# A decision-tree stage with attention threaded through it: the next group's attention one tree earlier

## Chip, core and metric

One core of a Trainium2 chip runs the whole program. The metric is the time of one execution on the device in microseconds (us); of the kernel before there are three runs, with their median. The profile is of one further execution.

## What is computed

`x` is 64 sequences of 128 rows of 128 features; `ctx` is 64 sequences of 120 rows. Four blocks follow each other, each adding to `x`; cut to what matters:

```python
x = x + cross_attention_0(layernorm(x), ctx)
x = x + mixture_of_8_experts(layernorm(x))          # top 1, and a shared expert
x = x + cross_attention_1(layernorm(x), ctx)        # softmax(q k / sqrt(128)) v
x = x + trees(layernorm(x))

def trees(x):                                       # 8 trees of depth 7, 255 nodes each
    logits = x @ W_in.T + b_in                      # 8 * 255 columns
    decisions = logits > 0
    on_path = one_hot of the 8 nodes that the decisions lead through, per tree
    return (silu(logits) * on_path) @ W_out.T
```

The layer norm in front of the second attention is called norm 3 here, the one in front of the trees norm 4 (LN4).

## The kernel before

The 64 sequences go through in 16 groups of four (`G = 4`, `W = 512` columns), so that a tile is 128 x 512 and fills one PSUM bank. A first stage does block 1 and the shared expert, a middle stage the routed experts. The last stage, `phase_c`, does the trees of group g and, between them, the second attention of group g + 1 and the norm 3 of group g + 2. It is the stage that the change touches. The group loop is unrolled for the first group and the last three, and a hardware loop of two groups a turn does the others.

**A tree on each engine.** Each group has 8 trees (`TREES`), counted by `p`, each of two chunks of 128 nodes.
- TensorE: `t_logits` gives the logits of both chunks, three 512-column matmuls each, since both operands are split into a high and a low part (`x4T_h`, `x4T_l`, `win_h`, `win_l`; lines L1009 to L1011). `t_path` adds two matmuls (L1018, L1020) of the decisions `dec` with constant matrices; they push the logit of every node off the path so far down that silu gives zero. `t_output` multiplies the masked activations with `W_out`, again split, in six matmuls (L1031 to L1033), all of a group into bank 4.
- VectorE: `t_decide` makes `dec` (L1430) of the first chunk's logits, one tree ahead; `t_low` makes the low halves `sil_l` = `sil` - `sil_h` (L1446).
- ScalarE: `t_silu_high` makes `sil` (L715) from the banks and its high halves `sil_h` (L723). For tree 1 VectorE makes the high halves. Even trees use banks 0 and 1, odd trees banks 2 and 3.

**The attention among them.** `c_scores` (L918) puts the scores in bank 7, `c_max_scores` and `c_softmax` (L654) make `prob1`, `c_turn_prob` turns it with four TensorE transposes (the helper `turn`, L758) into bank 5, `c_pT_evac` (L660) copies it to `prob1T`, `c_values` (L933) multiplies it with V into bank 6, and `c_attended` on VectorE (L1336, L1338, L1343) scales and adds it to X. `c_stats4` (L1079, L1084), `rstd` on GpSimd (L490, L492) and `c_norm4` (L1090) give the normalised rows `xn_c`. `c_turn_x4` turns them into bank 7, `c_x4_high` on ScalarE (L664) and `c_x4_low` on VectorE (L1358) split them into `x4T_h` and `x4T_l`, which the logits of the next group read. `c_stats3`, `c_norm3`, `c_turn_x` and `c_xnT_evac` (L650) do the like for norm 3 of group g + 2, through the same `xn_c` and bank 5. The output sum of a group is evacuated (`accT`, L729), turned into bank 6 in tree 3 of the group after and added to X by `t_result` (L1452).

**What sets the order.** Each engine has its own program, written out by hand: `c_body` of each engine says after which tree's step which piece of attention stands. An engine works its list in this order; between engines there are semaphore waits alone. SyncE only stores the results in this stage, and GpSimd does `rstd` and gathers the routed rows of group g + 3.

In `c_body` of TensorE the order in tree p is: logits of tree p + 1, path of tree p, output of tree p - 1. In tree 7 the first logits of the next group stand at the end. That is, between path 6 and output 6 there are output 5 and path 7 in either kernel, and in the one before the turn of norm 4's rows as well:

```python
if p == 7 and not last(g, 1):
    c_turn_x4(g + 1)
t_path(g, p)
...
if p:
    t_output(g, p - 1)
...
if p == TREES - 1 and not last(g, 1):
    t_logits(g + 1, 0)
```

Of the kernel before, what the change touches and what calls it, by code (L numbers as in the profile page):

```python
# [15 lines left out]
P = 128  # L16
# [4 lines left out]
W = G * P  # L21
# [52 lines left out]
def program(nc, x, ctx_kv, ctx_t, w0, b0, gate, sh_gate, sh_up, sh_down, rt_gate, rt_up, rt_down,  # L74
# [5 lines left out]
    with ExitStack() as ctx:  # L80
# [12 lines left out]
        V = sb("V", [KEYS, B * P])  # L93
# [38 lines left out]
        srec = sb("srec", [P, G])  # L132
# [26 lines left out]
        def bank(i, n=512, parts=P):  # L159
            return PS[0:parts, 512 * i:512 * i + n]  # L160
# [118 lines left out]
        def cols(a, start, n):  # L279

            return a[:, start:start + n] if isinstance(start, int) else a[:, bass.ds(start, n)]

        def tile(a, j, n=P):
            return a[:, j * n:(j + 1) * n]
# [16 lines left out]
        def below(g, n):  # L301

            return isinstance(g, int) and g < n

        def last(g, n):

            return isinstance(g, int) and g >= NG - n
# [23 lines left out]
        def c_bank(h, n, b):  # L331

            return 7 if below(h, n) else b
# [251 lines left out]
        def _(act):  # L585
# [145 lines left out]
            def c_body(g, u, stores):  # L731

                for p in range(TREES):
                    if p == 7 and not last(g, 1):
                        c_x4_high(g + 1)
                    t_silu_high(g, p)
                    if p == 0 and not first(g):
                        t_acc_evac(g - 1)
                    if not last(g, 1):
                        if p == 1:  # L740
                            c_softmax(g + 1)
                        if p == 3:
                            c_pT_evac(g + 1)
                    if not last(g, 2):
                        if p == 5:
                            c_xnT_evac(g + 2)
# [6 lines left out]
        def _(pe):  # L753

            def turn(dst, src, rows, n, signal):

                for j in range(G):
                    i = pe.transpose(dst[0:n, j * rows:(j + 1) * rows], tile(src, j, n), IDENT[0:rows, 0:rows])  # L758
                i.then_inc(signal, 1)
# [149 lines left out]
            def c_turn_x(h):  # L909
                pe.wait_ge(c_xn3, h + 1)  # L910
                if below(h, 2) and h:
                    pe.wait_ge(c_x4l, h)
                turn(bank(c_bank(h, 2, 5)), xn_c, P, P, c_xnT_ps)

            def c_scores(h):
# [6 lines left out]
            def c_turn_prob(h):  # L922
                pe.wait_ge(c_exp, h + 1)
                turn(bank(c_bank(h, 1, 5), W, KEYS), prob1, P, KEYS, c_pT_ps)

            def c_values(h):
                pe.wait_ge(c_pT, h + 1)
                if first(h):
                    pe.wait_ge(a_vb, V_POOL)
                if not below(h, 2):  # L930
                    pe.wait_ge(t_res, h - 1)
                for j in range(G):
                    i = pe.matmul(tile(bank(c_bank(h, 1, 6)), j), tile(prob1T, j), cols(V, h * W + j * P, P),  # L933
                                  start=True, stop=True)
                i.then_inc(c_pv_ps, 1)

# [99 lines left out]
            def c_body(g, u, stores):  # L1036
                for p in range(TREES):
                    if p == 3 and not first(g):
                        pe.wait_ge(c_x3, g + 1)
                        pe.wait_ge(t_accT, g)  # L1040
                        turn(bank(6), accT, P, P, t_acc)
                    if p + 1 < TREES:
                        t_logits(g, p + 1)
                    if p == 7 and not last(g, 1):
                        c_turn_x4(g + 1)
                    t_path(g, p)
                    if not last(g, 1):
                        if p == 0:
                            c_scores(g + 1)
                        if p == 3:  # L1050
                            c_turn_prob(g + 1)
                        if p == 4:
                            c_values(g + 1)
                    if not last(g, 2):
                        if p == 5:
                            c_turn_x(g + 2)
                    if p:
                        t_output(g, p - 1)
                    elif not first(g):
                        t_output(g - 1, TREES - 1)  # L1060
                    if p == TREES - 1 and not last(g, 1):
                        t_logits(g + 1, 0)

# [10 lines left out]
        def _(dve):  # L1074
# [259 lines left out]
            def c_attended(h):  # L1334
                dve.wait_ge(c_exp, h + 1)
                dve.tensor_reduce(ssum[:, :], by_tile(prob1, KEYS), AX.X, ALU.add).then_inc(c_sum, 1)  # L1336
                dve.wait_ge(c_sum, h + 1)
                dve.reciprocal(srec[:, :], ssum[:, :]).then_inc(c_rec, 1)  # L1338
                dve.wait_ge(c_rec, h + 1)
                dve.wait_ge(c_pv_ps, h + 1)  # L1340
                for j in range(G):
                    row = cols(X, h * W + j * P, P)
                    i = dve.scalar_tensor_tensor(out=row, in0=tile(bank(c_bank(h, 1, 6)), j), scalar=srec[:, j:j + 1],  # L1343
                                                 in1=row, op0=ALU.mult, op1=ALU.add)
                i.then_inc(c_x3, 1)

# [9 lines left out]
            def c_x4_low(h):  # L1356
                dve.wait_ge(c_x4h, h + 1)
                dve.tensor_tensor(x4T_l, bank(7), x4T_h.bitcast(F32), ALU.subtract).then_inc(c_x4l, 1)  # L1358
# [95 lines left out]
            def c_body(g, u, stores):  # L1454
                for p in range(TREES):
                    if p:
                        t_low(g, p - 1)
                    elif not first(g):
                        t_low(g - 1, TREES - 1)
                    if p + 1 < TREES:  # L1460
                        t_decide(g, p + 1)
                    elif not last(g, 1):
                        c_x4_low(g + 1)
                        t_decide(g + 1, 0)
                    if p == 3 and not first(g):
                        t_result(g - 1, 1 - u, stores)
                    if not last(g, 1):
                        if p == 1:
                            c_max_scores(g + 1)
                        if p == 4:  # L1470
                            c_attended(g + 1)
                        if p == 5:
                            c_stats4(g + 1)
                        if p == 6:
                            c_norm4(g + 1)
                    if not last(g, 2):
                        if p == 0:
                            c_add_routed(g + 2, u)
                        if p == 2:
                            c_stats3(g + 2)  # L1480
                        if p == 3:
                            c_norm3(g + 2)

            t_decide(0, 0)
            phase_c(dve, c_body)
# [42 lines left out]
```

## Time and profile before

| | |
|---|---|
| median of 3 runs | 867.29 us (867.15 to 867.87) |
| the profiled execution | 868.49 us |
| its span, first to last instruction | 866.7 us |
| last stage, from about | 385 us on |
| TensorE busy over the span | 794.8 us (92%) |
| VectorE | 653.7 us (75%) |
| ScalarE | 539.0 us (62%) |
| GpSimd | 272.3 us (31%) |

PE is TensorE and PEld its weight loads, which run beside its matmuls; DVE is VectorE, ACT ScalarE, POOL GpSimd. Matmuls are pipelined: each row's duration overlaps the next row's, so the distance between two starts is what a matmul costs. The same holds in part for VectorE and ScalarE, where an instruction starts a little ahead of the recorded end of the one before. A bracket at a row's end gives the time the engine was idle before it and who ended that.

### The profile page before, as it was taken

The numbers are of one execution on the slowest core, as the hardware profiler recorded it, in microseconds if no ns is written. First come the engines' busy times: TensorE is split into PE (matmuls) and PEld (weight loads), VectorE is DVE, ScalarE is ACT, GpSimd is POOL, SyncE is SP. The second block draws the span as 40 slices with busy tenths as digits, with TensorE's granted clock in tenths as the row PEclk, the third lists the DMA queues.
The fourth block names the chain that finished last, engine by engine and source line by source line (L and its number), as shares of the span: only waits on it lengthen the run. The fifth ranks groups of instructions, "written<-read, shape, count | busy, mean of one in ns | idle before, by whom it ended". The sixth has DMA issues, their size and how long they took to land.

```text
span 866.7 us, 15372 instructions
## 1 busy us (share of the span) xinstructions
PE 794.8 (92%) x4488; PEld 639.0 (74%) x4489; DVE 653.7 (75%) x1728; ACT 539.0 (62%) x944; POOL 272.3 (31%) x341
## 2 busy tenths in 40 slices
PE   5999996877769958999999999999999999999997
PEld 3788885766569958987777777777777777777775
DVE  5788887866585527669888888988888888888774
ACT  2577675554223313437777776877777777768765
POOL 1332331488437717013213222321331232121000
PEclk8999999999799979999999999999999999999999
DMA  6346773533314424210000000000000000000000
GB/s 147 95 119 193 204 211 106 169 102 97 110 49 146 145 76 113 80 50 13 19 7 25 24 0 24 24 24 1 24 24 15 9 24 24 0 24 13 13 1 25
DMA packets 91426, 55.72 MB, mean 64 GB/s; under 512 B 13439, under 2 KB 88183, under 8 KB 91255
## 3 DMA queue, kind: packets, MB, share of 16 engines
q1 hardware_dynamic: 74304, 40.38, 16.6%
q0 software_dynamic: 4096, 8.40, 3.4%
q10 hardware_dynamic: 12983, 6.41, 2.7%
q8 instruction: 22, 0.36, 0.2%
q14 instruction: 21, 0.17, 0.1%
HBM read 32.10 MB, written 23.07 MB: 64 GB/s over the span
## 4 chain that ended last, share of the span: by engine, by line
PE 34%; DVE 22%; ACT 13%; issue 12%; POOL 12%; DMA 4%; ACTq 1%; DVEq 1%; POOLq 0%; SPq 0%
POOL x_sorted L507 5%; PE PS L758 4%; DVE sil_l L1446 4%; DVE dec L1430 3%; DVE xn_c L1090 3%; PE PS L1009 3%; POOL rs L492 3%; PE PS L1011 3%; PE PS L1010 3%; PE PS L773 3%; ACT sil L715 2%; PE PS L1031 2%; PE PS L1033 2%; PE PS L1032 2%; ACT L715 2%
## 5 line engine op out<-in xcount | busy, mean ns | idle before, releaser
L715 ACT ACTIVATE sil<-PS,b_in_c 128x512 f32<-128x512 f32 x256 | 162.2, 686 | 113.3 <-PE PS L1018 108.3
L1446 DVE TENSOR_TENSOR sil_l<-sil,sil_h 128x512 fp32r<-128x512 f32 x256 | 164.7, 684 | 44.7 <-ACT sil_h L723 44.2
L490 POOL TENSOR_TENSOR ve<-mv,eps 128x4 f32<-128x4 f32 x64 | 17.6, 276 | 458.4 <-DVE mv L1084 458.3
L723 ACT ACTIVATE sil_h<-sil 128x512 fp32r<-128x512 f32 x224 | 128.9, 631 | 0.0
L1031 PE MATMUL PS<-sil_h,wout_l 128*128 128x512 f32 x256 | 117.2, 458 | 1.6 <-DVE sil_l L1446 1.6
L1430 DVE TENSOR_SCALAR dec<-PS,b_in_c 128x512 bf16<-128x512 f32 x128 | 95.4, 746 | 26.2 <-PE PS L1011 26.2
L1009 PE MATMUL PS<-x4T_h,win_l 128*128 128x512 f32 x256 | 102.2, 399 | 2.0 <-ACT yo L675 0.7
L1033 PE MATMUL PS<-sil_h,wout_h 128*128 128x512 f32 x256 | 100.4, 392 | 0.0
L1032 PE MATMUL PS<-sil_l,wout_h 128*128 128x512 f32 x256 | 100.4, 392 | 0.0
L1011 PE MATMUL PS<-x4T_h,win_h 128*128 128x512 f32 x256 | 99.9, 390 | 0.0
L1010 PE MATMUL PS<-x4T_l,win_h 128*128 128x512 f32 x256 | 99.9, 390 | 0.0
L773 PE MATMUL PS<-xsT,w_now 128*128 128x128 f32 x640 | 80.4, 279 | 7.8 <-DVE ract L1366 7.6
L773 PEld LDWEIGHTS PS<-xsT,w_now 128*128 128x128 f32 x640 | 75.2, 193 | 10.4 <-issue 7.0
L548 POOL DMA_INDIRECT ys<-y_sorted,idx x64 | 72.8, 1138 | 28.3 <-issue 15.2
L507 POOL DMA_INDIRECT x_sorted<-xs,idx x64 | 64.9, 1014 | 25.4 <-issue 14.8
L492 POOL TENSOR_TENSOR rs<-ve,neg_half 128x4 f32<-128x4 f32 x64 | 70.1, 1095 | 5.0
L1031 PEld LDWEIGHTS PS<-sil_h,wout_l 128*128 128x128 f32 x256 | 48.3, 189 | 18.9 <-DVE sil_l L1446 6.6
L1009 PEld LDWEIGHTS PS<-x4T_h,win_l 128*128 128x128 f32 x256 | 48.0, 187 | 17.4 <-issue 3.7
L1079 DVE BATCH_NORM_STATS2 st<-X 128x6 f32<-128x128 f32 (+1 forms) x256 | 55.4, 279 | 7.0 <-DMA X<-in_x 4.0
L1033 PEld LDWEIGHTS PS<-sil_h,wout_h 128*128 128x128 f32 x256 | 48.0, 188 | 10.7
L1011 PEld LDWEIGHTS PS<-x4T_h,win_h 128*128 128x128 f32 x256 | 48.0, 188 | 10.4
L1148 DVE COPY w_now<-WGU 128x512 f32 x80 | 33.6, 462 | 28.8 <-PE PS L773 26.6
(165 smaller groups left out, 1564.2 us busy)
## 6 DMA issues: line engine op xcount, KB each, us to landing
x_sorted<-zeros SPq DMA_DIRECT2D x4, 1280.0 KB, 6.8
xs_in<-x_sorted SPq DMA_DIRECT2D x20, 256.0 KB
y_sorted<-yo ACTq DMA_DIRECT2D x20, 256.0 KB, 2.5
X<-in_x SPq DMA_DIRECT2D x16, 256.0 KB, 2.8
rows<-xn SPq DMA_DIRECT2D x16, 256.0 KB, 2.5
xs<-rows SPq DMA_DIRECT2D x16, 256.0 KB, 3.0
out<-res SPq DMA_DIRECT2D x16, 256.0 KB, 2.4
ctxT<-in_ctx_t SPq DMA_DIRECT2D x16, 240.0 KB, 3.2
```

Of the source, the lines that this page charges most:

```text
L507: pool.indirect_dma_start(x_sorted[h], bass.IndirectOffsetOnAxis(ap=idx[:, v, j:j + 1], axis=0), tile(xs[v], j), None).then_inc(scattered[ ...
L715: act.activation(tile(sil[p % 2], c, W), bank(2 * (p % 2) + c), ACT.Silu, bias=b_in_c[:, 2 * p + c:2 * p + c + 1]).then_inc(t_silu, 1)
L723: act.activation(tile(sil_h[p % 2], c, W), tile(sil[p % 2], c, W), ACT.Copy).then_inc(t_hi, 1)
L773: i = pe.matmul(tile(bank(1 + 2 * v + t), n), tile(w_now[v], 2 * FC * t + n), tile(xsT[u], 2 * v + t), start=True, stop=True)
L1009: pe.matmul(dst, lo, x4T_h, start=True, stop=False, skip_group_check=True)
L1010: pe.matmul(dst, hi, x4T_l, start=False, stop=False, skip_group_check=True)
L1011: i = pe.matmul(dst, hi, x4T_h, start=False, stop=True, skip_group_check=True)
L1031: pe.matmul(bank(4), lo, act_h, start=(p == 0 and c == 0), stop=False)
L1032: pe.matmul(bank(4), hi, act_l, start=False, stop=False)
L1033: pe.matmul(bank(4), hi, act_h, start=False, stop=(p == TREES - 1 and c == 1)).then_inc(t_out, 1)
L1430: dve.tensor_scalar(dec[p % 2], bank(2 * (p % 2)), b_in_c[:, 2 * p:2 * p + 1], 0.0, ALU.add, ALU.is_gt).then_inc(t_dec, 1)
L1446: dve.tensor_tensor(tile(sil_l[p % 2], c, W), tile(sil[p % 2], c, W), tile(sil_h[p % 2], c, W).bitcast(F32), ALU.subtract).then_inc(t_lo, 1)
```

## The change

It moves pieces of attention in the lists of TensorE, ScalarE and VectorE; no instruction is added or dropped, and GpSimd's and SyncE's lists stay as they are. Scores and softmax stay where they were.

- TensorE: the turn of the probabilities goes from tree 3 (ahead of output 2) to the end of tree 2; the values from tree 4 to tree 3, and into bank 5; the turn of norm 4's rows from tree 7 to tree 6, ahead of path 6. Three semaphore waits change with the banks: `c_turn_x` now waits until `c_attended` has read bank 5 (`c_x3`), accT's turn waits for `t_result` of the group before last, and `c_values` waits for neither.
- ScalarE: the evacuation of the turned probabilities goes from tree 3 to tree 2, that of the turned norm 4 rows from ahead of tree 7's silu to ahead of tree 6's.
- VectorE: attended from tree 4 to tree 3, norm 3 from tree 3 to tree 4, statistics 4 from tree 5 to tree 4, norm 4 from tree 6 to tree 5, the low half of x4T from tree 7 to tree 6.

```diff
@@ ScalarE, c_body
-                    if p == 7 and not last(g, 1):
+                    if p == 6 and not last(g, 1):
                         c_x4_high(g + 1)
                     t_silu_high(g, p)
...
-                        if p == 3:
+                        if p == 2:
                             c_pT_evac(g + 1)
@@ TensorE, c_turn_x
+                if not below(h, 2):
+                    pe.wait_ge(c_x3, h)
                 turn(bank(c_bank(h, 2, 5)), xn_c, P, P, c_xnT_ps)
@@ TensorE, c_values
-                if not below(h, 2):
-                    pe.wait_ge(t_res, h - 1)
                 for j in range(G):
-                    i = pe.matmul(tile(bank(c_bank(h, 1, 6)), j), tile(prob1T, j), cols(V, h * W + j * P, P),
+                    i = pe.matmul(tile(bank(c_bank(h, 1, 5)), j), tile(prob1T, j), cols(V, h * W + j * P, P),
@@ TensorE, c_body
                     if p == 3 and not first(g):
-                        pe.wait_ge(c_x3, g + 1)
+                        if not below(g, 2):
+                            pe.wait_ge(t_res, g - 1)
                         pe.wait_ge(t_accT, g)
                         turn(bank(6), accT, P, P, t_acc)
                     if p + 1 < TREES:
                         t_logits(g, p + 1)
-                    if p == 7 and not last(g, 1):
+                    if p == 6 and not last(g, 1):
                         c_turn_x4(g + 1)
                     t_path(g, p)
                     if not last(g, 1):
                         if p == 0:
                             c_scores(g + 1)
                         if p == 3:
-                            c_turn_prob(g + 1)
-                        if p == 4:
                             c_values(g + 1)
...
+                    if p == 2 and not last(g, 1):
+                        c_turn_prob(g + 1)
                     if p == TREES - 1 and not last(g, 1):
                         t_logits(g + 1, 0)
@@ VectorE, c_attended
-                    i = dve.scalar_tensor_tensor(out=row, in0=tile(bank(c_bank(h, 1, 6)), j), scalar=srec[:, j:j + 1],
+                    i = dve.scalar_tensor_tensor(out=row, in0=tile(bank(c_bank(h, 1, 5)), j), scalar=srec[:, j:j + 1],
@@ VectorE, c_body (behind t_low and t_decide of each tree)
                     elif not last(g, 1):
-                        c_x4_low(g + 1)
                         t_decide(g + 1, 0)
                     if p == 3 and not first(g):
                         t_result(g - 1, 1 - u, stores)
-                    if not last(g, 1):
-                        if p == 1:
-                            c_max_scores(g + 1)
-                        if p == 4:
-                            c_attended(g + 1)
-                        if p == 5:
-                            c_stats4(g + 1)
-                        if p == 6:
-                            c_norm4(g + 1)
                     if not last(g, 2):
                         if p == 0:
                             c_add_routed(g + 2, u)
                         if p == 2:
                             c_stats3(g + 2)
+                        if p == 4:
+                            c_norm3(g + 2)
+                    if not last(g, 1):
+                        if p == 1:
+                            c_max_scores(g + 1)
                         if p == 3:
-                            c_norm3(g + 2)
+                            c_attended(g + 1)
+                        if p == 4:
+                            c_stats4(g + 1)
+                        if p == 5:
+                            c_norm4(g + 1)
+                        if p == 6:
+                            c_x4_low(g + 1)
```

**Place 1, TensorE, trees 6 and 7 of the first group.** L1018 and L1020 are a path pair (`dec0` of tree 6, `dec1` of tree 7), L1031 to L1033 output matmuls (`sil_h1` of tree 5, `sil_h0` of tree 6), L758 the turn of norm 4's rows. Before:

```order
L1011 MATMUL PS<-x4T_h_112,win_h_53 128x512
L1018 MATMUL PS<-dec0_121,anc_in 128x512
L1020 MATMUL PS<-dec0_121,anc_lv 128x512
L1031 MATMUL PS<-sil_h1_115,wout_l_52 128x512
...
L1033 MATMUL PS<-sil_h1_115,wout_h_54 128x512
L758 MATMUL PS<-WA,xn_c_108 128x128 x4
L1018 MATMUL PS<-dec1_122,anc_in 128x512
L1020 MATMUL PS<-dec1_122,anc_lv 128x512
L1031 MATMUL PS<-sil_h0_114,wout_l_52 128x512
```

And with the change:

```order
L1011 MATMUL PS<-x4T_h_112,win_h_53 128x512
L758 MATMUL PS<-WA,xn_c_108 128x128 x4
L1018 MATMUL PS<-dec0_121,anc_in 128x512
L1020 MATMUL PS<-dec0_121,anc_lv 128x512
L1031 MATMUL PS<-sil_h1_115,wout_l_52 128x512
...
L1033 MATMUL PS<-sil_h1_115,wout_h_54 128x512
L1018 MATMUL PS<-dec1_122,anc_in 128x512
L1020 MATMUL PS<-dec1_122,anc_lv 128x512
L1031 MATMUL PS<-sil_h0_114,wout_l_52 128x512
```

The turn has left the stretch between path 6 and output 6, where six output matmuls of tree 5 and path 7 remain.

**Place 2, VectorE, trees 3 to 5 of a group behind the loop.** L1446 (now L1447) are the low halves of trees 2, 3 and 4 in turn, L1452 (L1453) is the result. Before:

```order
L1452 TENSOR_TENSOR res0_123<-X,PS 128x512
L1090 TENSOR_SCALAR xn_c_108<-X,mv,rs 128x128 x4
L1446 TENSOR_TENSOR sil_l1_117<-sil1_119,sil_h1_115 128x512 x2
L1430 TENSOR_SCALAR dec1_122<-PS,b_in_c 128x512
L1336 TENSOR_REDUCE ssum<-prob1_111 128x4
L1338 RECIPROCAL srec<-ssum 128x4
L1343 SCALAR_TENSOR_TENSOR X<-PS,srec,X 128x128 x4
L1446 TENSOR_TENSOR sil_l0_116<-sil0_118,sil_h0_114 128x512 x2
L1430 TENSOR_SCALAR dec0_121<-PS,b_in_c 128x512
L1079 BN_STATS st<-X 128x6 x4
L1084 BN_AGGR mv<-st 128x2 x4
```

And with the change:

```order
L1453 TENSOR_TENSOR res0_123<-X,PS 128x512
L1337 TENSOR_REDUCE ssum<-prob1_111 128x4
L1339 RECIPROCAL srec<-ssum 128x4
L1344 SCALAR_TENSOR_TENSOR X<-PS,srec,X 128x128 x4
L1447 TENSOR_TENSOR sil_l1_117<-sil1_119,sil_h1_115 128x512 x2
L1431 TENSOR_SCALAR dec1_122<-PS,b_in_c 128x512
L1091 TENSOR_SCALAR xn_c_108<-X,mv,rs 128x128 x4
L1080 BN_STATS st<-X 128x6 x4
L1085 BN_AGGR mv<-st 128x2 x4
L1447 TENSOR_TENSOR sil_l0_116<-sil0_118,sil_h0_114 128x512 x2
```

Between the low halves of tree 2 and those of tree 4 stand the same pieces as before and the statistics of norm 4 besides.

**Place 3, ScalarE, trees 5 to 7 of the first group.** L715 is silu, L723 the high halves. Before:

```order
L723 ACTIVATE sil_h1_115<-sil1_119 128x512 x2
L650 ACTIVATE xn3T_109<-PS 128x512
L715 ACTIVATE sil0_118<-PS,b_in_c 128x512 x2
L723 ACTIVATE sil_h0_114<-sil0_118 128x512 x2
L664 ACTIVATE x4T_h_112<-PS 128x512
L715 ACTIVATE sil1_119<-PS,b_in_c 128x512 x2
```

And with the change:

```order
L723 ACTIVATE sil_h1_115<-sil1_119 128x512 x2
L650 ACTIVATE xn3T_109<-PS 128x512
L664 ACTIVATE x4T_h_112<-PS 128x512
L715 ACTIVATE sil0_118<-PS,b_in_c 128x512 x2
L723 ACTIVATE sil_h0_114<-sil0_118 128x512 x2
L715 ACTIVATE sil1_119<-PS,b_in_c 128x512 x2
```

The evacuation of x4T_h now stands ahead of tree 6's silu.

## Rows read from the trace of the kernel before

**Rows 1.** Stretches of 30 us: busy us of each engine, granted clock, DMA.

```profile
core 0: us, PE busy (x) PEld busy (x) DVE busy (x) ACT busy (x) POOL busy (x), PEclk, DMA share, GB/s
...
594.00:624.00 30.00, 29.67 (x146) 22.36 (x145) 25.43 (x61) 22.68 (x39) 8.07 (x9) 1.00 0.06 17
```

**Rows 2.** Timeline of TensorE's matmuls: start, us, engine, line, operation.

```profile
600.40 0.39 PE L1018 MATMUL PS<-dec,anc_in 128*128 128x512 bf16 x1
...
605.40 0.60 PE L758 MATMUL PS<-WA,accT 128*128 128x128 f32 x4
606.06 0.50 PE L1009 MATMUL PS<-x4T_h,win_l 128*128 128x512 f32 x1
606.40 0.40 PE L1010 MATMUL PS<-x4T_l,win_h 128*128 128x512 f32 x1
...
608.01 0.60 PE L758 MATMUL PS<-WA,prob 128*120 128x128 f32 x4
...
608.68 0.40 PE L1032 MATMUL PS<-sil_l,wout_h 128*128 128x512 f32 x1
...
611.62 1.06 PE L933 MATMUL PS<-V,prob1T 120*128 x8
...
612.76 0.40 PE L1032 MATMUL PS<-sil_l,wout_h 128*128 128x512 f32 x1
...
618.90 0.39 PE L1018 MATMUL PS<-dec,anc_in 128*128 128x512 bf16 x1
...
621.15 0.66 PE L758 MATMUL PS<-WA,xn_c 128*128 128x128 f32 x4 [0.27 <-DVE xn_c L1090]
621.64 0.38 PE L1018 MATMUL PS<-dec,anc_in 128*128 128x512 bf16 x1
...
623.45 0.46 PE L1009 MATMUL PS<-x4T_h,win_l 128*128 128x512 f32 x1
...
630.38 0.39 PE L1018 MATMUL PS<-dec,anc_in 128*128 128x512 bf16 x1
```

**Rows 3.** Timeline of TensorE's weight loads.

```profile
606.06 0.19 PEld L1009 LDWEIGHTS PS<-x4T_h,win_l 128*128 128x128 f32 x1 [0.30 <-ACT sil L715]
...
621.14 0.42 PEld L758 LDWEIGHTS PS<-WA,xn_c 128*128 128x128 f32 x4 [0.69 <-DVE xn_c L1090]
...
621.89 0.19 PEld L1031 LDWEIGHTS PS<-sil_h,wout_l 128*128 128x128 f32 x1 [0.15 <-DVE sil_l L1446]
```

**Rows 4.** Timeline of VectorE.

```profile
607.14 1.29 DVE L1446 TENSOR_TENSOR sil_l<-sil,sil_h 128x512 fp32r<-128x512 f32 x2 [1.18 <-ACT sil_h L723]
...
609.01 0.68 DVE L1452 TENSOR_TENSOR res<-X,PS 128x512 f32<-128x512 f32 x1
609.61 1.11 DVE L1090 TENSOR_SCALAR xn_c<-X,mv,rs 128x128 f32 x4
610.63 1.29 DVE L1446 TENSOR_TENSOR sil_l<-sil,sil_h 128x512 fp32r<-128x512 f32 x2
...
612.50 0.64 DVE L1336 TENSOR_REDUCE ssum<-prob 128x4 f32<-128x480 f32 x1
...
614.54 1.28 DVE L1446 TENSOR_TENSOR sil_l<-sil,sil_h 128x512 fp32r<-128x512 f32 x2
...
616.40 0.86 DVE L1079 BATCH_NORM_STATS2 st<-X 128x6 f32 x4
...
617.70 1.26 DVE L1446 TENSOR_TENSOR sil_l<-sil,sil_h 128x512 fp32r<-128x512 f32 x2
...
619.98 1.11 DVE L1090 TENSOR_SCALAR xn_c<-X,mv,rs 128x128 f32 x4 [0.36 <-POOL rs L492]
621.15 1.29 DVE L1446 TENSOR_TENSOR sil_l<-sil,sil_h 128x512 fp32r<-128x512 f32 x2
```

**Rows 5.** Timeline of ScalarE.

```profile
606.48 1.15 ACT L723 ACTIVATE sil_h<-sil 128x512 fp32r<-128x512 f32 x2
...
619.33 1.27 ACT L715 ACTIVATE sil<-PS,b_in_c 128x512 f32<-128x512 f32 x2 [0.85 <-PE PS L1018]
620.49 1.15 ACT L723 ACTIVATE sil_h<-sil 128x512 fp32r<-128x512 f32 x2
621.84 0.60 ACT L664 ACTIVATE x4T_h<-PS 128x512 fp32r<-128x512 f32 x1 [0.21 <-PE PS L758]
622.34 1.26 ACT L715 ACTIVATE sil<-PS,b_in_c 128x512 f32<-128x512 f32 x2
```

**Rows 6.** The page's costliest groups: one low half on VectorE, mean ns.

```profile
L1446 DVE TENSOR_TENSOR sil_l<-sil,sil_h 128x512 fp32r<-128x512 f32 x256 | 164.7, 684 | 44.7 <-ACT sil_h L723 44.2
```

## The prediction

> **What bounds the kernel now.** Times of one group are given in us behind its mark, the start of tree 1's path matmuls; in the group read here 600.40 us [rows 2]; a change under about 0.2% (1.7 us) could not be told from none.
>
> I read the table by stretches first, since the change touches the last stage alone. It shows TensorE busy for 29.67 of 30 us in a middle stretch at granted clock 1.00, with VectorE at 25.43, ScalarE at 22.68 and GpSimd at 8.07 [rows 1]. TensorE bounds the stage; the question is which of its waits go and which come. So next the timeline of TensorE, and only the starts: between 600.40 and 605.40 stand 22 matmuls of 512 columns, 5.00 us, hence 0.2273 each [rows 2]. In that coin a tree's logits or output (6 matmuls) cost 1.365, its path pair 0.455. A turn of four tiles costs 608.68 - 608.01 less one matmul, 0.44, and the attention's values 612.76 - 611.62 less one, 0.91; the scores, eight passes of the same kind, I take the same. A group is 8 x (1.365 + 0.455 + 1.365) + 4 x 0.44 + 2 x 0.91 = 29.06 us of work. It takes 630.38 - 600.40 = 29.98 [rows 2]: 0.92 us a group is waiting. It lies in three places:
> - Behind the turn of accT the weights of the next logits stand idle 0.30 for silu of tree 2 [rows 3].
> - The turn of LN4's rows should start at 618.90 + 0.455 + 1.365 = 620.72 and starts at 621.15, as VectorE's xn_c, begun 619.98, itself waited on GpSimd [rows 2, 4]: 0.43, and 0.05 more since the turn then takes 0.49.
> - From 623.45 to 630.38 are 26 matmuls and the scores, 6.82 of work in 6.93: 0.11, where the next group's first logits wait for the low half of x4T.
>
> **The change part by part, in steady state.** Nothing is added to or taken from any engine: the same instructions stand in another order, and no DMA moves. GpSimd's code is untouched.
>
> *Turned probabilities with tree 2.* The turn now stands ahead of accT's, at 5.00. Both take 0.88, so the logits of tree 4 come at 5.88. Silu of tree 2 has its first half before then: sil_h of tree 2 starts at 6.08, and two halves of silu stand 1.16 before it (that distance is seen at tree 6, 619.33 to 620.49), so its first half starts at 4.92 and is done at 5.61 [rows 5]. The first 0.30 is hidden: a gain, if it stays one.
>
> *Values with tree 3.* Evacuating the turned probabilities follows sil_h of tree 2 on ScalarE: 6.08 + 1.15 + one activation of 0.60 = 7.83 [rows 5], where TensorE is ready at 5.88 + 1.365 + 0.455 = 7.70. Bound for this wait: 0 to 0.2, I take 0.13. Bank 5 instead of 6 costs nothing of its own: the values need the evacuated copy anyway. The waits that come with it are long met: the result of two groups back, and for the turn of norm 3's rows at 14.98 the read of bank 5, which ends at 11.25 (both below).
>
> *VectorE between trees 2 and 4.* This is where the order bites first. Low half of tree 2 starts at 6.74, after waiting for ScalarE [rows 4], so nothing earlier helps it. Behind it, by distances between starts [rows 4]: low half and decision 1.87, result 0.60, attended 2.04, low half and decision 1.87, norm 3 1.02, statistics 1.30. Before, the statistics stood behind tree 4's low half; now they are ahead of it, which starts at 6.74 + 1.87 + 0.60 + 2.04 + 1.87 + 1.02 + 1.30 = 15.44, where it stood at 14.14. Its first half takes 0.68 [rows 6], the step to TensorE's weights 0.05 (621.84 to 621.89), and the load that then stands open 0.11 (606.06 to 606.40 less a matmul; a load itself is 0.19) [rows 2, 3, 4]. Output of tree 4 can start at 16.28. TensorE's own work would have it there at 5.88 + 3 x 1.365 (logits 4 to 6) + 3 x 0.455 (paths 3 to 5) + 0.91 (values) + 2 x 1.365 (outputs 2 and 3) + 0.44 (turn of the rows of norm 3) = 15.42. **A wait of 0.86 that was not there**; the gain of 0.30 and the 0.13 at the values vanish in it, since VectorE's chain, not TensorE's, now sets this point.
>
> *Turn of LN4's rows with tree 6.* Statistics end about where tree 4's low half starts. Before, xn_c began 619.98 - 617.70 = 2.28 after that point, GpSimd's two steps between; now at 15.44 + 2.28 = 17.72, done 1.11 later, 18.83 [rows 4]. TensorE arrives after output 4 and logits 7, at 16.28 + 2.73 = 19.01. The turn no longer waits: the 0.48 is gone, with 0.18 to spare.
>
> *What stands between path 6 and output 6.* This is the term I trust most. Output 6 needs a chain through two engines. In the trace before: path 6 at 618.90, silu 619.33, sil_h 620.49, low half 621.15 with its first half done 621.84, weights 621.89 [rows 2 to 5]. That is 2.99, and the weights were idle 0.15 for it: it was just covered, and by what? Path 6, output 5 and path 7 are 2.275; the rest of the cover was the turn of LN4's rows (0.44) and its own wait (0.48). The change takes both away from there. Worse, ScalarE now evacuates x4T_h ahead of tree 6's silu: 0.69 behind the turn's start, and the next activation 0.50 behind that [rows 5], so silu starts 1.19 after the turn, where path 6 alone would allow 0.44 + 0.43. From the turn: 1.19 + 1.16 + 0.66 + 0.68 + 0.16 = 3.85, so output 6 starts at 19.01 + 3.85 = 22.86. TensorE is ready at 19.01 + 0.44 + 2.275 = 21.73. **A second new wait, 1.13.** VectorE is no hindrance: low half of tree 5, decision 7 and x4T's low half are done before 22.0.
>
> *First logits of the next group.* x4T's low half is ready early: the 0.11 goes.
>
> **Sum.** 22.86 + output 6 (1.365) + 6.82 = 31.05 to the next mark, against 29.98: +1.07 a group. The old waits of 0.92 are gone, 0.86 and 1.13 come. The cycle closes, since the softmax chain that sets 6.74 starts from path 1. There are 15 hand-overs. The first lacks accT's turn and a result; I count it like the rest. The last has no norm 3, so tree 4's low half comes 1.02 sooner, its wait mostly goes, and I count 0.5. 14 x 1.07 + 0.5 = 15.5. Against the profiled execution, 868.49 us around a span of 866.7, that gives 884.0; the runs' median, 867.29, stands 1.2 below it, so 882.8, say **883**.
>
> **A rule weighed.** The weights stood 0.30, 0.69 and 0.15 us idle in one group for named producers [rows 3], and the rows price that at 0.92 of 29.98. The Trainium skill (Perfetto Trace Analysis, Optimization Strategy) says to find the gaps on the bounding engine, see what releases them and make that start sooner. Followed for the turn and the logits behind it alone, it makes this change a gain of the first rival's size, 858.4. The trace agrees as far as the idle times go; the 0.15 row is what speaks against it here.
>
> **The rivals.**
> - *The removed waits stay removed* (the other side). Place: output 6. If sil_l of tree 6 were ready when TensorE arrives, the turn's 0.48 and the logits' 0.11 would be won on 15 groups, -8.9: 858.4. It decides where chain and open load take less than 2.275 from path 6; 2.99 before any delay by x4T_h is measured. With no wait at output 4, 0.13 at the values and two thirds of the new wait here (0.75), it would come to about no change. For it: VectorE has 4.5 us of slack in 30 [rows 1]. Chance of a gain 0.04, of no change 0.03.
> - *Only output 6 waits.* If VectorE gets to tree 4's low half in time, waits are 0.13 and 1.13, against 0.92: +0.34 a group, 5.1 in all, 872.4. It needs VectorE to be 0.8 faster over 8.7 us of steps that follow each other without a gap in these rows. Chance 0.13.
> - *The turn waits too.* 0.18 is all there is to spare. If GpSimd is held up by 0.6 at the power, or VectorE's longer queue adds as much, output 6 goes back by 0.4: 14 x 0.4 more, 888.6. GpSimd's part of the 2.28 is read beside a low half on VectorE, and is beside one again. Chance 0.10.
> - *The clock falls.* The granted clock is 1.00 (2.4 GHz) in a stretch that holds waits up to 0.48 [rows 1]; new ones are 0.9 and 1.1. If each group ran one tree at 1.2 GHz, 14 x 0.2273 = 3.2 us on 15 groups, 48: 931. Chance 0.02. The Trainium skill (TensorE: Matmul & The Clock Gate, A second HAM failure mode) tells of short idles between groups of matmuls that make the clock swing; no trace here has it in this stage.
>
> **How the numbers follow.** The forecast has 0.68. Its own spread: open loads at nothing (2 x 0.11) and VectorE's steps 0.1 quicker take 14 x 0.32 = 4.5 off, 878; loads at their full 0.19 (2 x 0.08) and VectorE 0.1 later add 14 x 0.26 = 3.6, 886.5. With the second rival's 872.4 below and the third's 888.6 above, the range is 872 to 889. Slower by over 0.2%: 0.68 + 0.13 + 0.10 + 0.02 = 0.93; faster 0.04, the same 0.03.
>
> **What would show it.** TensorE's waits should list output for sil_l of VectorE as the largest, near 1 us on most groups, at trees 4 and 6, and no turn waiting for xn_c. The stretches should show TensorE about 1 us less busy in 30, every other engine's sum in the stage unchanged, and the distance between two marks 31.0. I am wrong if output 4 starts on time (VectorE's order cheaper than its sum), or if sil_l of tree 6 comes less than 3 us behind path 6.

## The result, and the profile after

The changed kernel takes 882.58 us (median of 4 runs, 881.76 to 882.87) where the kernel before takes 867.58 beside it: a ratio of 1.0174, 95% interval 1.0161 to 1.0187. It is slower by 15.0 us; 883 was forecast. The profiled execution took 882.51 us around a span of 880.7.

The page's busy times of the changed kernel, for the whole span:

```profile
PE 796.3 (90%) x4488; PEld 636.9 (72%) x4489; DVE 652.5 (74%) x1728; ACT 536.9 (61%) x944; POOL 269.5 (31%) x341
```

No engine does more than before: VectorE 652.5 against 653.7, ScalarE 536.9 against 539.0, and TensorE's 796.3 against 794.8 is for the same 4488 matmuls, of which one that follows a wait is recorded longer (0.50 us at 629.25 below, 0.39 for the ones behind it). The 14.0 us of span are idle time. The stretches of 30 us (busy us of each engine, granted clock, DMA) say where:

```profile
core 0: us, PE busy (x) PEld busy (x) DVE busy (x) ACT busy (x) POOL busy (x), PEclk, DMA share, GB/s
594.00:624.00 30.00, 28.95 (x142) 21.48 (x141) 24.66 (x59) 21.83 (x36) 7.66 (x9) 1.00 0.07 17
624.00:654.00 30.00, 28.95 (x142) 21.62 (x141) 24.55 (x60) 21.66 (x37) 6.97 (x10) 1.00 0.06 17
```

TensorE was busy 29.67 of such a stretch [rows 1] and is now at 28.95, with the clock still at 1.00. Who is waited for is named by the list of TensorE's waits from 385 us on (engine, line, waited for: us in total, times, longest):

```profile
PE PS L1031 <- DVE sil_l L1447: 16.8, 31, 0.8
PE PS L1009 <- ACT yo L675: 0.7, 1, 0.7
PE PS L758 <- ACT accT L729: 0.7, 1, 0.7
```

Before, that list had the turn waiting for xn_c at its head:

```profile
PE PS L758 <- DVE xn_c L1090: 2.4, 11, 0.3
PE PS L1031 <- DVE sil_l L1446: 1.6, 4, 0.6
```

The turn has left the list; output, waiting for VectorE's low half, stands there 31 times. The timeline of TensorE over one group shows both places. Its mark, path 1, is at 606.57:

```profile
606.57 0.39 PE L1018 MATMUL PS<-dec,anc_in 128*128 128x512 bf16 x1
...
611.57 0.60 PE L758 MATMUL PS<-WA,prob 128*120 128x128 f32 x4
612.00 0.60 PE L758 MATMUL PS<-WA,accT 128*128 128x128 f32 x4
...
613.85 0.39 PE L1018 MATMUL PS<-dec,anc_in 128*128 128x512 bf16 x1
614.42 1.15 PE L933 MATMUL PS<-V,prob1T 120*128 x8
...
621.90 0.60 PE L758 MATMUL PS<-WA,xn_c 128*128 128x128 f32 x4
622.73 0.50 PE L1031 MATMUL PS<-sil_h,wout_l 128*128 128x512 f32 x1 [0.23 <-DVE sil_l L1447]
623.07 0.39 PE L1032 MATMUL PS<-sil_l,wout_h 128*128 128x512 f32 x1
...
625.57 0.60 PE L758 MATMUL PS<-WA,xn_c 128*128 128x128 f32 x4
626.00 0.38 PE L1018 MATMUL PS<-dec,anc_in 128*128 128x512 bf16 x1
...
627.82 0.39 PE L1018 MATMUL PS<-dec,anc_in 128*128 128x512 bf16 x1
...
629.25 0.50 PE L1031 MATMUL PS<-sil_h,wout_l 128*128 128x512 f32 x1 [0.82 <-DVE sil_l L1447]
629.59 0.39 PE L1032 MATMUL PS<-sil_l,wout_h 128*128 128x512 f32 x1
```

Their weight loads:

```profile
622.72 0.19 PEld L1031 LDWEIGHTS PS<-sil_h,wout_l 128*128 128x128 f32 x1 [0.47 <-DVE sil_l L1447]
...
629.25 0.19 PEld L1031 LDWEIGHTS PS<-sil_h,wout_l 128*128 128x128 f32 x1 [1.31 <-DVE sil_l L1447]
```

Output 4 stands at 622.73, output 6 at 629.25. After path 7 at 627.82 output 6 could stream from 628.28, and it does from 629.59 less one matmul of 0.23, 629.36: 1.08 us late. It is the same, 1.08 or 1.09, at all 15 hand-overs. The second turn of xn_c, norm 4's, follows the last of logits 7 without a gap. Next to it VectorE's timeline, which made both:

```profile
613.30 1.30 DVE L1447 TENSOR_TENSOR sil_l<-sil,sil_h 128x512 fp32r<-128x512 f32 x2 [1.17 <-ACT sil_h L723]
...
617.82 1.28 DVE L1447 TENSOR_TENSOR sil_l<-sil,sil_h 128x512 fp32r<-128x512 f32 x2
...
619.68 1.11 DVE L1091 TENSOR_SCALAR xn_c<-X,mv,rs 128x128 f32 x4
620.71 0.87 DVE L1080 BATCH_NORM_STATS2 st<-X 128x6 f32 x4
...
622.01 1.26 DVE L1447 TENSOR_TENSOR sil_l<-sil,sil_h 128x512 fp32r<-128x512 f32 x2
...
624.30 1.12 DVE L1091 TENSOR_SCALAR xn_c<-X,mv,rs 128x128 f32 x4 [0.36 <-POOL rs L492]
...
627.19 0.68 DVE L1359 TENSOR_TENSOR x4T_l<-PS,x4T_h 128x512 fp32r<-128x512 f32 x1
628.50 1.29 DVE L1447 TENSOR_TENSOR sil_l<-sil,sil_h 128x512 fp32r<-128x512 f32 x2 [0.63 <-ACT sil_h L723]
```

From tree 2's low half at 613.30 to tree 4's at 622.01 VectorE waits for no other engine: there it is the late one. At tree 6's low half, 628.50, it had been idle 0.63 for sil_h: there the chain through ScalarE is late.

The distance between the turns of accT gives the group. The first and the fourteenth in the kernel before, then in the changed one:

```profile
425.94 0.60 PE L758 MATMUL PS<-WA,accT 128*128 128x128 f32 x4
...
814.77 0.60 PE L758 MATMUL PS<-WA,accT 128*128 128x128 f32 x4
```

```profile
426.13 0.60 PE L758 MATMUL PS<-WA,accT 128*128 128x128 f32 x4
...
828.73 0.60 PE L758 MATMUL PS<-WA,accT 128*128 128x128 f32 x4
```

On the average of 13 that is 29.91 us before and 30.97 with the change. The difference is 13 x 1.06 = 13.8. From the stage's first matmul (385.39 before, 384.77 with the change) to the first of these turns is 41.36 instead of 40.55, 0.8 more, and from the fourteenth turn to the fifteenth it is 28.67 us against 28.64. (The turn of the probabilities now lies ahead of accT's, so that one of it, 0.44, counts in the first stretch and no longer in the last. By the path 1 marks the first hand-over grew by 0.38, 390.35 to 420.70 against 390.97 to 420.94, and the last by 0.46, 823.30 to 852.40 against 809.77 to 838.41.) The last stage grew by 14.6 and began 0.6 earlier in this execution, which leaves the 14.0 of the span.

### The profile page after: what moved, and what is told of

Its sections match the earlier page's. It is cut to its first block, busy times and chain, and to the rows that moved or that the text cites. A ratio compares the mean times of both kernels' runs of the same rounds, so it can differ in the third digit from the quotient of the medians.

```text
span 880.7 us, 15372 instructions
## 1 busy us (share of the span) xinstructions
PE 796.3 (90%) x4488; PEld 636.9 (72%) x4489; DVE 652.5 (74%) x1728; ACT 536.9 (61%) x944; POOL 269.5 (31%) x341
## 4 chain that ended last, share of the span: by engine, by line
PE 50%; DVE 18%; POOL 9%; issue 8%; ACT 8%; DMA 4%; ACTq 1%; DVEq 0%; POOLq 0%; SPq 0%
PE PS L1031 5%; PE PS L1009 5%; PE PS L1011 5%; PE PS L758 5%; PE PS L1010 5%; POOL x_sorted L507 5%; PE PS L1032 4%; PE PS L1033 4%; DVE sil_l L1447 4%; PE PS L773 3%; PE PS L781 2%; DVE dec L1431 2%; DMA x_sorted<-xs,idx 2%; ACT sil L715 2%; PE PS L1018 2%
## 5 line engine op out<-in xcount | busy, mean ns | idle before, releaser
L715 ACT ACTIVATE sil<-PS,b_in_c 128x512 f32<-128x512 f32 x256 | 162.0, 686 | 109.4 <-PE PS L1018 106.9
L1447 DVE TENSOR_TENSOR sil_l<-sil,sil_h 128x512 fp32r<-128x512 f32 x256 | 164.6, 684 | 50.9 <-ACT sil_h L723 50.9
L1031 PE MATMUL PS<-sil_h,wout_l 128*128 128x512 f32 x256 | 117.9, 461 | 16.8 <-DVE sil_l L1447 16.8
L723 ACT ACTIVATE sil_h<-sil 128x512 fp32r<-128x512 f32 x224 | 129.1, 633 | 0.0
L1033 PE MATMUL PS<-sil_h,wout_h 128*128 128x512 f32 x256 | 100.5, 393 | 0.0
L1031 PEld LDWEIGHTS PS<-sil_h,wout_l 128*128 128x128 f32 x256 | 48.2, 188 | 45.2 <-DVE sil_l L1447 32.5
L548 POOL DMA_INDIRECT ys<-y_sorted,idx x64 | 69.1, 1080 | 28.3 <-issue 15.2
L1033 PEld LDWEIGHTS PS<-sil_h,wout_h 128*128 128x128 f32 x256 | 48.1, 188 | 10.8
L1010 PEld LDWEIGHTS PS<-x4T_l,win_h 128*128 128x128 f32 x256 | 48.1, 188 | 9.8
```

The costliest lines, as they stand in the source:

```text
L715: act.activation(tile(sil[p % 2], c, W), bank(2 * (p % 2) + c), ACT.Silu, bias=b_in_c[:, 2 * p + c:2 * p + c + 1]).then_inc(t_silu, 1)
L723: act.activation(tile(sil_h[p % 2], c, W), tile(sil[p % 2], c, W), ACT.Copy).then_inc(t_hi, 1)
L1010: pe.matmul(dst, hi, x4T_l, start=False, stop=False, skip_group_check=True)
L1031: pe.matmul(bank(4), lo, act_h, start=(p == 0 and c == 0), stop=False)
L1033: pe.matmul(bank(4), hi, act_h, start=False, stop=(p == TREES - 1 and c == 1)).then_inc(t_out, 1)
L1447: dve.tensor_tensor(tile(sil_l[p % 2], c, W), tile(sil[p % 2], c, W), tile(sil_h[p % 2], c, W).bitcast(F32), ALU.subtract).then_inc(t_lo, 1)
```

## The experiments

A group's length is worked out the same way for each: the distance of the first and the fourteenth turn of accT, over 13. Each time is a median beside the kernel before on the same chip, which stood at 867.58 beside the change and at 867.46 to 867.75 in the three sets of experiments.

| kernel | median us | ratio to before, 95% | group, us |
|---|---|---|---|
| before | 867.6 | | 29.91 |
| the change | 882.58 | 1.0161 to 1.0187 | 30.97 |
| late turn (turn and split back in tree 7) | 872.16 | 1.0040 to 1.0074 | 30.29 |
| row sums in tree 2 | 875.03 | 1.0067 to 1.0101 | 30.39 |
| next logits first | 871.37 | 1.0032 to 1.0055 | 30.24 |
| both edits | 858.06 | 0.9881 to 0.9914 | 29.37 |
| values alone, on before | 867.24 | 0.9985 to 1.0007 | 29.89 |
| late split (split alone back in tree 7) | 878.70 | 1.0104 to 1.0138 | 30.74 |
| path 7 first (on both edits) | 857.96 | 0.9876 to 0.9909 | 29.30 |
| row sums in tree 2, on before | 866.72 | 0.9974 to 0.9999 | 29.85 |

The theory: two waits, each behind another engine, take the place of three that went. The rivals: all the loss is VectorE's order (A); all of it is the hand-over of norm 4's rows (B).

**The late turn.** One part undone, on all three engines:

```diff
-                    if p == 6 and not last(g, 1):
+                    if p == 7 and not last(g, 1):
                         c_x4_high(g + 1)
...
-                    if p == 6 and not last(g, 1):
+                    if p == 7 and not last(g, 1):
                         c_turn_x4(g + 1)
...
                     elif not last(g, 1):
+                        c_x4_low(g + 1)
                         t_decide(g + 1, 0)
...
-                        if p == 6:
-                            c_x4_low(g + 1)
```

> The changed kernel with one part undone: the turn of norm 4's rows, its evacuation and the low half of x4T are back in tree 7. Theory of two waits (VectorE's order delays output 4; the hand-over through ScalarE and VectorE delays output 6): output 4 still starts at 16.3 behind the mark, the turn covers part of the chain behind path 6 again, so output 6 waits about 0.4 instead of 1.1 and the first logits again 0.1. A group takes 30.4 instead of 31.0, the kernel about 874. Rival A (all the loss is VectorE's order): no change, 882.6. Rival B (all the loss is the hand-over): back to about 867.5.

Measured 872.16, a group 30.29: two thirds of the loss goes. Both rivals fall, A since it moved, B since 4.5 us stay. The timeline of this kernel's weight loads:

```profile
646.73 0.19 PEld L1031 LDWEIGHTS PS<-sil_h,wout_l 128*128 128x128 f32 x1 [0.45 <-DVE sil_l L1447]
...
652.56 0.19 PEld L1031 LDWEIGHTS PS<-sil_h,wout_l 128*128 128x128 f32 x1 [0.46 <-DVE sil_l L1447]
```

The first is output 4, unchanged (0.47 in the changed kernel's). The second is output 6: 0.46 idle, where the changed kernel has 1.31. The matmuls of output 6 are 0.23 late there, where 0.4 was forecast, and those of output 5 are 0.16 late, which was not forecast.

**Row sums in tree 2.** VectorE's sum and reciprocal for the softmax need only the exponentials; they move to where VectorE waits for sil_h anyway:

```diff
-            def c_attended(h):
+            def c_row_sums(h):
                 dve.wait_ge(c_exp, h + 1)
                 dve.tensor_reduce(ssum[:, :], by_tile(prob1, KEYS), AX.X, ALU.add).then_inc(c_sum, 1)
                 dve.wait_ge(c_sum, h + 1)
                 dve.reciprocal(srec[:, :], ssum[:, :]).then_inc(c_rec, 1)
+
+            def c_attended(h):
                 dve.wait_ge(c_rec, h + 1)
...
+                        if p == 2:
+                            c_row_sums(g + 1)
```

> The changed kernel with the row sums of the probabilities and their reciprocal (about 1.0 us of VectorE between the low halves of trees 2 and 4) made in tree 2, where VectorE was idle. Theory of two waits: output 4 starts on time at 15.5, the wait of 0.86 goes, the one at output 6 stays at 1.1; a group takes 30.3, the kernel about 873. Rival A (all is VectorE's order): back to 867.5 or below. Rival B (all is the hand-over): no change, 882.6.

Measured 875.03, a group 30.39 against 30.3 forecast. Its waits:

```profile
PE PS L1031 <- DVE sil_l L1450: 13.8, 18, 0.8
PE PS L758 <- ACT accT L729: 0.7, 1, 0.7
PE PS L1009 <- ACT yo L675: 0.7, 1, 0.7
```

31 waits have become 18; 15 of them are output 6, about 0.8 each, and the other three stand at the start and the end of the stage. Output 4 is on time, output 6 is not.

**Next logits first.** The early turn makes x4T ready by the end of output 5, so the next group's first logits can stand where every other tree's logits do, and output 6 behind them:

```diff
                     if p + 1 < TREES:
                         t_logits(g, p + 1)
+                    elif not last(g, 1):
+                        t_logits(g + 1, 0)
...
-                    if p == TREES - 1 and not last(g, 1):
-                        t_logits(g + 1, 0)
```

> The changed kernel with the next group's first logits ahead of path 7 and output 6, in the order of all other trees; the early turn makes this possible. Theory of two waits: sil_l of tree 6 is then ready before TensorE comes to output 6 (22.9 against 23.2), the wait of 1.1 goes but for 0.1 for the low half of x4T, the one at output 4 stays; a group takes 30.0, the kernel about 868.5. Rival A: no change, 882.6. If the delay of silu by the evacuation is larger than thought, output 6 would still wait and the kernel stand above 870.

Measured 871.37, a group 30.24: the wait at output 6 is gone, but 0.2 a group more stay than forecast. The timeline of the weight loads shows where:

```profile
647.93 0.19 PEld L1031 LDWEIGHTS PS<-sil_h,wout_l 128*128 128x128 f32 x1 [0.46 <-DVE sil_l L1447]
...
653.33 0.19 PEld L1009 LDWEIGHTS PS<-x4T_h,win_l 128*128 128x128 f32 x1 [0.56 <-ACT sil L715]
```

Output 4 waits as in the changed kernel. The logits' weights at 653.33 wait for the low half of x4T, which VectorE has at 652.40 + 0.68 = 653.08. (The row names silu of tree 6, which those logits wait for too; the half of it that the first three need is done by 651.90 + 0.69 = 652.59.) I had counted 0.1 for this step, it takes 0.25 and the open load behind it.

**Both edits.** The two diffs above together:

> Both edits at once. Theory: both waits are gone, what is left of 29.06 us of work is 0.13 at the values and at most 0.1 at the first logits; a group takes 29.3, the kernel about 857.4, faster than the kernel before by 10. If a third wait comes up behind the two (GpSimd's power ahead of norm 4, or ScalarE's table loads ahead of silu of tree 2), a group stays near 29.6 or above and the kernel near 862.

Measured 858.06: 1.0% faster than the kernel before (0.9 to 1.2%), and by the medians 2.8% faster than the changed one. Neither edit does it alone; each leaves one wait of the two. Its waits from 385 us on:

```profile
PE PS L1031 <- DVE sil_l L1450: 1.4, 3, 0.6
PE PS L758 <- ACT accT L729: 0.7, 1, 0.7
```

**Values alone.** On the kernel before, the probabilities turned with tree 2 and the values with tree 3, nothing else (on ScalarE the evacuation goes to tree 2 likewise, the banks and their waits are those of the change):

```diff
                         if p == 3:
-                            c_turn_prob(g + 1)
-                        if p == 4:
                             c_values(g + 1)
...
+                    if p == 2 and not last(g, 1):
+                        c_turn_prob(g + 1)
```

> The kernel before with one part of the change alone: the probabilities are turned with tree 2, the values stand with tree 3 in bank 5; VectorE's order, the turn of norm 4's rows and its split stay as before. Theory (a gain on TensorE that the next late piece takes back): the wait for silu of tree 2, 0.3, goes and about 0.15 at the values comes, but the turn of norm 4's rows still waits for xn_c, which hangs on VectorE and GpSimd alone; a group stays at 29.9 and the kernel at 867.7 within 1. Rival (TensorE's waits add up): a group 0.15 shorter, the kernel about 865.5. Rival 2 (the shift itself costs): above 870.

Measured 867.24, no difference. Its waits:

```profile
PE PS L758 <- DVE xn_c L1091: 5.1, 15, 0.6
PE PS L1031 <- DVE sil_l L1447: 1.4, 3, 0.6
```

The turn waited 2.4 us in 11 times before and waits 5.1 in 15 here. TensorE came sooner and stood longer, there and at the values: the gain of 0.3 at silu of tree 2 is worth nothing by itself.

**Late split.** The changed kernel, turn in tree 6, with its evacuation on ScalarE behind the silu of tree 6 and the low half in tree 7 (two of the first experiment's three moves):

```diff
-                    if p == 6 and not last(g, 1):
+                    if p == 7 and not last(g, 1):
                         c_x4_high(g + 1)
...
                     elif not last(g, 1):
+                        c_x4_low(g + 1)
                         t_decide(g + 1, 0)
```

> The changed kernel with the turn of norm 4's rows in tree 6, but its evacuation on ScalarE and the low half of x4T back in tree 7. Theory: silu of tree 6 then starts 0.43 behind path 6 instead of 0.75, sil_l of tree 6 comes 0.3 sooner, output 6 waits 0.8 instead of 1.1; a group takes 30.65 and the kernel about 878. Rival (the evacuation ahead of silu costs nothing, it is the missing cover alone): no change, 882.6. If the late low half of x4T holds the next group's first logits, above 879.

Measured 878.70, a group 30.74. The weights of output 6 idle 1.04 instead of 1.31. So of the 1.1 us at output 6 about 0.3 is the evacuation ahead of silu, and the rest the missing cover. A few hundredths of it come back at the next group's first logits, whose weights idle 0.16 there, so that a group gains 0.23.

**Path 7 first.** On the version with both edits, path 7 moved ahead of the next group's logits:

```diff
-                    elif not last(g, 1):
-                        t_logits(g + 1, 0)
                     if p == 6 and not last(g, 1):
                         c_turn_x4(g + 1)
                     t_path(g, p)
+                    if p == TREES - 1 and not last(g, 1):
+                        t_logits(g + 1, 0)
```

> The version with both edits, 858.1, but with path 7 ahead of the next group's first logits, output 6 behind both. Its group took 29.37 against 29.06 of work; the runs of it show the first logits start 0.27 behind the end of the low half of x4T. Path 7 (0.455) in front covers that: a group takes 29.15, the kernel about 855. Rival (decision 7 is late, so path 7 waits instead): no gain, 858.

Measured 857.96, the same, as the rival had it; only the distance between the turns, 29.30 against 29.37, shows a gain. The rival's reason does not hold, though: in its trace path 7 of a group starts at 644.43, 0.24 behind the last matmul of output 5 (644.19), so it does not wait for decision 7, and the first logits behind it do not wait either. The size was wrong. In the version with both edits the weights of those logits were idle before:

```profile
643.78 0.19 PEld L1009 LDWEIGHTS PS<-x4T_h,win_l 128*128 128x128 f32 x1 [0.25 <-issue]
```

This 0.25 I had taken for TensorE's loss. The matmuls of output 5 were still streaming in most of it; 0.07 was the loss.

**Row sums in tree 2, on the kernel before.** The same edit as above, without the change:

```diff
                         if p == 1:
                             c_max_scores(g + 1)
+                        if p == 2:
+                            c_row_sums(g + 1)
                         if p == 4:
                             c_attended(g + 1)
```

It takes away what made norm 4's turn late, and so asks what that wait was worth:

> The kernel before with one edit: row sums and reciprocal in tree 2, so that VectorE comes to norm 4 earlier and the turn of its rows no longer waits for xn_c. It tells what that wait was worth. Theory (the wait was cover for the chain silu, sil_h, sil_l behind path 6): the turn's 0.48 goes, output 6 waits 0.35 to 0.4 in its place; a group takes 29.8 instead of 29.9, the kernel about 866. Rival (the wait is worth what it shows, as in the prediction's first rival): 0.48 on 15 groups, the kernel about 860.5.

Measured 866.72, a ratio of 0.9974 to 0.9999, and a group 29.85 against 29.91. The turn follows on time, and the weights of output 6 say what took its place:

```profile
621.59 0.19 PEld L1031 LDWEIGHTS PS<-sil_h,wout_l 128*128 128x128 f32 x1 [0.64 <-DVE sil_l L1449]
```

And its matmuls, the first row being the second one of path 7:

```profile
621.07 0.38 PE L1020 MATMUL PS<-dec,anc_lv 128*128 128x512 bf16 x1
621.60 0.50 PE L1031 MATMUL PS<-sil_h,wout_l 128*128 128x512 f32 x1
621.93 0.39 PE L1032 MATMUL PS<-sil_l,wout_h 128*128 128x512 f32 x1
```

The weights idled 0.15 before [rows 3] and idle 0.64 now. Output 6 streams from 621.93 - 0.23 = 621.70 and could have from 621.07 + 0.23 = 621.30: 0.40 late. What it replaces is the turn's 0.48 in the group of [rows 2]; the loop takes two groups a turn, and in the other one it was 0.36 (the turn at 651.04 behind a matmul at 650.51, path 7 at 651.54). So about 0.42 a group was removed, 0.40 came, and of it all 0.06 a group was won. The rival's 860.5 is far outside.

## Why the prediction was right

It went by starts behind the mark, and these can be laid beside the trace after:

| step | forecast | measured |
|---|---|---|
| low half of tree 4 starts | 15.44 | 15.44 |
| output 4 streams | 16.28 | 16.27 |
| xn_c of norm 4 starts | 17.72 | 17.73 |
| turn of norm 4's rows | 19.01 | 19.00 |
| output 6 streams | 22.86 | 22.79 |
| next mark | 31.05 | 30.96 |

- *VectorE between trees 2 and 4.* Right. The wait shown at output 4 itself is 622.84 - 622.34 = 0.50, not 0.86: the rest of TensorE's lateness lies ahead of it, at the values (0.12, and 0.08 more in the values themselves), at output 3 (0.08) and in the matmuls between. It makes no difference where it lies, since VectorE sets this point. The row sums in tree 2 take the 0.50 away, and with it 0.58 a group (30.97 to 30.39). They also make the case of the second rival, only output 6 waiting: it was priced at 872.4 and takes 875.03.
- *The turn no longer waits.* Right; it stands 0.15 behind the end of xn_c on this group (625.42 to 625.57), and the load of its weights starts 0.05 behind that end, so 0.10 was to spare and the third rival was never far.
- *Path 6 to output 6.* Right, 1.08 against 1.13. That this is cover lost, and not a cost of the turn's new place, is shown from two sides: put back into tree 7 the turn covers again; and on the kernel before, where the turn was made punctual without being moved, the wait came up in its place. The part of the evacuation was argued as 0.32 and measured as 0.23 a group (30.97 to 30.74).
- *Values.* 0.13 forecast, 0.12 measured, and absorbed. The trace of before had no such row; the bound by ScalarE's rows sufficed. A term is missing, though: from their start to that of the output behind them the values take 0.91 before (611.62 to 612.76 less one matmul) and 0.99 with the change (614.42 to 615.64 less one), in every group. The prediction had "Bank 5 instead of 6 costs nothing of its own"; whether the 0.08 is the bank's or comes of the weights, which are now loaded only when the values start, no run separates. Here it vanishes in the wait at output 4.
- *The first and the last hand-over.* The last is right: 0.5 forecast, 0.46 measured by the marks. The first was counted "like the rest", 1.07, and grew by 0.38: no wait came at output 4, and before the change the weights of output 6 already stood idle 0.70 there (412.61). This and 13 x 0.01 make up nearly all of the 0.9 us between the forecast rise of 15.5 in the last stage and the 14.6 that it grew by.
- *The length of a group.* The rise came out, 1.07 forecast and 1.06 measured, but both ends were too high by 0.07 to 0.09: the group read before was the longer of the loop's two, 29.98 where the average is 29.91, and the next mark came at 30.96 and not 31.05. Within that pair of groups the rise is 0.98. That the two cancel is luck.
- *The stretches.* TensorE is 0.72 less busy in 30 us, where about 1 was forecast; at output 4 and 6 only 0.23 and 0.82 are recorded as idle, the rest of each wait lies in the longer record behind it.
- *The rule weighed.* The Trainium skill (Perfetto Trace Analysis, Optimization Strategy) says to find the gaps and make what releases them start sooner or finish faster. The turn's gap was closed by itself on the kernel before and brought 0.06 us a group: the runs agree with the rule only when the next chain to arrive is looked at together with the gap. With that chain taken out of the way as well, the same early turn is part of a kernel that is 1.0% faster.
- *The clock* stayed at 1.00 with waits of 1.08; that rival fell.

What stays open: the version with both edits and path 7 first has 29.30 us a group against 29.06 by count. Of these 0.24, 0.12 is the wait at the values (630.99 for 630.87 in the version with both edits, the same with path 7 first) and 0.08 to 0.09 the longer values themselves. Why the values take longer was not tested.

## What to carry to other kernels

Before closing a gap on the bounding engine, look for the next thing that the engine will need, and reckon when that is ready if the gap were gone: the gap may only be covering another wait that comes up in its place. Such a chain can be reckoned from distances between starts on each engine, laid out in the new order: here that put every step of the table within 0.1 us, though not the first hand-over. And where work is taken out of the stretch that covers a chain, put other work in: here the next group's logits, for which the early turn had just made room.

## What had not been expected of the hardware

TensorE's weights follow the end of VectorE's low half of sil by 0.05 us (621.84 to 621.89, [rows 3, 4]), but the end of the low half of x4T by 0.25 and 0.27 (653.08 to 653.33 with the next logits first; 642.82 + 0.69 = 643.51 to 643.78 with both edits). The logits there wait on more semaphores than the outputs do; whether that is the reason was not tried. And idle time of the weight loads is not idle time of the matmuls: 0.25 of the one was 0.07 of the other with both edits, 0.64 was 0.40 with the row sums early on the kernel before, and 1.31 was 1.08 in the changed kernel.
